# A two-layer cross-attention and expert network: padded tails, no mask matmul in the second scores, and a new order of steps

## The reference

```python
x = x + L0_xattn(layernorm(x), ctx)            # 16 heads of 8, over all 1601 keys
x = x + L0_ffn(layernorm(x))                   # 9 experts of width 352, top 2 of sigmoid scores
x = x + L1_xattn(layernorm(x), ctx, indices)   # 64 indices a query, values 0..255
x = x + L1_ffn(layernorm(x))                   # 8 experts of width 176 (top 2) + a shared one
```

## Time and profile before

| | us |
|---|---|
| median of 3 runs (lowest, highest) | 1853.64 (1852.64, 1859.54) |
| the profiled execution | 1856.58 |
| its span, first to last instruction | 1854.6 |
| PE busy in the span | 1582.5 (85%) |
| DVE, ACT, POOL busy | 1103.3, 805.9, 738.4 |
| mean granted TensorE clock, share of full speed | 0.92 |

### The profile page before, as it was taken

One profiled execution on the slowest core, in us unless ns is written; L12 is line 12 of the kernel. 1 busy time (PEld: TensorE's weight loads), 2 busy tenths in 40 slices (PEclk: granted clock), 3 DMA queues, 4 the chain that ended last, 5 costly groups with the idle time before them and its releaser, 6 DMA issues.

```text
span 1854.6 us, 34408 instructions
## 1 busy us (share of the span) xinstructions
PE 1582.5 (85%) x12939; PEld 869.8 (47%) x13006; DVE 1103.3 (59%) x2509; ACT 805.9 (43%) x1214; POOL 738.4 (40%) x1145
## 2 busy tenths in 40 slices
PE   3289798889988898889998898889988798899667
PEld 3133363346633574336633574345733465347425
DVE  3276476546766576556766476655766477655323
ACT  2146426651366425671366524661266524672211
POOL 0336305741178214771168313771058412750140
PEclk8589799988999999999999999997999999999757
DMA  6310300022000300012000200012000200000000
GB/s 196 64 39 28 89 1 1 27 48 46 1 10 19 67 26 1 18 38 50 15 10 20 67 26 1 18 34 44 26 1 28 56 15 1 2 14 4 1 0 3
DMA packets 64853, 53.65 MB, mean 29 GB/s; under 512 B 14762, under 2 KB 57140, under 8 KB 64692
## 3 DMA queue, kind: packets, MB, share of 16 engines
q1 hardware_dynamic: 64692, 51.47, 11.4%
HBM read 38.98 MB, written 12.46 MB: 28 GB/s over the span
## 4 chain that ended last, share of the span: by engine, by line
PE 63%; DVE 10%; POOL 10%; ACT 5%; issue 5%; SPq 4%; DMA 3%; POOLq 0%; ACTq 0%; DVEq 0%
PE um L671 12%; PE um L660 9%; PE ob L604 8%; PE um L661 7%; PE um L576 5%; DVE mx L1022 4%; PE um L591 4%; POOL big L1236 3%; PE um L554 3%; DMA kst<-k_parts 2%; DVE mx L1127 2%; ACT probs L846 2%; PE um L645 2%; SPq L498 1%; PE um L712 1%
## 5 line engine op out<-in xcount | busy, mean ns | idle before, releaser
L1022 DVE TENSOR_REDUCE mx<-um 128x2 f32<-128x802 f32 (+1 forms) x512 | 504.9, 991 | 228.4 <-PE um L576 220.9
L846 ACT ACTIVATE probs<-um 128x1024 f32<-128x1024 f32 (+1 forms) x448 | 426.6, 963 | 228.0 <-PE um L591 221.6
L852 ACT ACTIVATE hid<-um 128x256 f32<-128x256 f32 (+3 forms) x328 | 125.5, 383 | 503.7 <-PE um L661 503.6
L604 PE MATMUL ob<-probs,vaug 128*9 128x256 f32 (+1 forms) x3328 | 286.9, 394 | 12.4 <-ACT oT L822 12.2
L1201 POOL TENSOR_TENSOR big<-iotab,idx_lo 128x512 bf16<-128x512 bf16 x256 | 266.0, 1055 | 14.7 <-PE um L748 9.5
L576 PE MATMUL um<-kst,qa 64*128 64x401 bf16 (+1 forms) x1024 | 184.2, 359 | 63.6 <-DMA kst<-k_parts 38.1
L1164 POOL CAST qst<-nm 128x4 bf16<-128x4 f32 x64 | 17.1, 268 | 470.9 <-DVE nm L1028 470.4
L591 PE MATMUL um<-big,kst 64*128 64x256 bf16 (+1 forms) x1664 | 173.0, 281 | 16.5 <-ACT big L892 4.6
L1040 DVE SCALAR_TENSOR_TENSOR x<-um,cw,x 128x128 f32<-128x128 f32 x288 | 87.7, 346 | 126.2 <-PE um L671 126.2
L1034 DVE TENSOR_TENSOR hid<-hid,um 128x256 f32<-128x256 f32 (+3 forms) x328 | 133.5, 412 | 24.2 <-ACT hid L852 22.8
L576 PEld LDWEIGHTS um<-kst,qa 64*128 64x128 bf16 x1024 | 50.1, 95 | 202.3 <-issue 65.8
(11 more groups left out here) (209 smaller groups left out, 2265.1 us busy)
## 6 DMA issues: line engine op xcount, KB each, us to landing
kst<-k_parts SPq DMA_DIRECT2D x384, 50.0 KB
k_parts<-big SPq DMA_DIRECT2D x72, 128.0 KB, 1.9
ctx_sb<-in_ctx SPq DMA_DIRECT2D x8, 768.0 KB
k1st<-k_parts SPq DMA_DIRECT2D x96, 32.0 KB
k_parts<-big SPq DMA_DIRECT2D x24, 64.0 KB, 1.6
kst<-in_L_ffn_w SPq DMA_DIRECT2D x1, 1408.0 KB
x<-in_x SPq DMA_DIRECT2D x8, 128.0 KB, 2.2
out<-x SPq DMA_DIRECT2D x8, 128.0 KB, 1.9
```

The source lines that it names most:

```text
L604: m = pe.matmul(ob[q:q + V1, 0:NQ], vaug[b % 2][0:kn, c, 2 * p + hh, :], probs[0:kn, (2 * (NGB * b + g) + hh) % NPS, (c % 2) * NQ:(c % 2 + ...
L846: act.activation(probs[0:kn, k:k + 2, 0:w], own_banks, ACT.Exp).then_inc(f_read, 1)
L852: act.activation(hid[0:nr, own % NHID, :], quarter[place[ev][0]][0:nr, 0:NQ], ACT.Silu).then_inc(th_ready, 1)
L1022: dve.tensor_reduce(mx[:, p % 2, s, :, j], pair[:, :, 0:w], AX, ALU.max, negate=True).then_inc(u_read, 1)
```

## The change

It has three parts. The second network's down projections read all 128 rows: `wd_sb` gets 9 tail slots in place of 5, zeros are written to them first (a DVE memset), the tail of an even expert stands in rows 0 to 47 and that of an odd one in rows 64 to 111 of its own slot; chunks are all 128 rows wide; `NHID` falls from 10 to 8. The mask matmuls of `s1` go; instead `mu` takes the minimum of exp and 3e38 and multiplies by the count (zero for rows not named) in one instruction, which DVE does and not POOL; `msk` no longer waits for the `s1` of the batch before. And the positions come from a table: R is 88.94; of batch 0 the first 8 `part` stand early and the others among its `s0`; the early `part` of later batches start at 54.3 (before: 56.4); the late ones stand 1.2 apart (before 1.34), each behind an `s0`; `key` 4 moves to 48.10 and `rel` 0 to 2 to 47.97, so that they change places on SP; the pairs of the last batch stand 1.495 apart.

```diff
-NEG = -1e30
+NEG, BIG = -1e30, 3e38
-NHID = 10
+NHID = 8
+AT = {'cl': 0.75, 'cl1': 0.75, 'y1': -0.803, 'turn': 2.997, 'early': 32, 'first': 8, 'side': 1, 'p0': -0.922, 'p0s': 1.05, 'pf': -2.88, 'pfs': 0.697, 'px': 0.0, 'pxs': 1.201, 'psn': 0.1, ...
...
-        wg_sb, wu_sb, wd_sb = (sb(n, [P, NE + NT1, P]) for n in ("wg_sb", "wu_sb", "wd_sb"))
+        wg_sb, wu_sb, wd_sb = (sb(n, [P, NE + k, P]) for n, k in (("wg_sb", NT1), ("wu_sb", NT1), ("wd_sb", NE)))
...
-            return P if e < NE else (SLOT + TAIL if 2 * (e - NE) + 1 < NE else TAIL)
+            return P
...
-            o = SLOT * (e % 2)
-            tail = NE + e // 2
-            return [(len(chunk0) + chunk1.index((1, e, 0)), 0, P, e), (len(chunk0) + chunk1.index((1, tail, 0)), o, o + TAIL, tail)]
+            return [(len(chunk0) + chunk1.index((1, k, 0)), 0, P, at) for k, at in ((e, e), (NE + e // 2, NE + e))]
...
+            def part_at(b, k):
+
+                own, prep = R * b, R * (b - 1)
+                if b == 0:
+                    return prep + Y1 + AT["p0"] + 0.5 * k if k < FIRST else own + AT["pf"] + AT["pfs"] * (k - FIRST)
+                if k < EARLY:
+                    return prep + Y1 + AT["p0"] + AT["p0s"] * (k - k % SIDE)
+                t = AT["px"] + AT["pxs"] * (k - EARLY)
+                return own + t - t % 1.0 + AT["psn"]
...
-                    put(prep + (48 if c < 3 else XL + 1.5), "rel", b, c)
+                    put(prep + (AT["rel"] if c < 3 else XL + AT["rel3"]), "rel", b, c)
...
-                    put(prep + Y1 + 1.4 + EARLY_STEP * k if k < EARLY else own + (43.0 / (NH0 - EARLY)) * (k - EARLY) + 0.1, "part", b, k)
+                    put(part_at(b, k), "part", b, k)
...
-                put(own + 46.5, "key", b, 4)
+                put(own + AT["kk1"], "key", b, 4)
...
+                step = AT["pair"] if b < NB - 1 else AT["pairl"]
                 for p in range(NP):
-                    for d, kind in ((0, "pair1"), (2.05, "q1"), (3.05, "s1"), (3.6, "mu"), (6.05, "w1"), (7.05, "c1")):
-                        put(chain + 8.7 + 4.4 * p + d, kind, b, p)
+                    for kind in ("pair1", "q1", "s1", "mu", "w1", "c1"):
+                        put(chain + AT["pair0"] + step * p + AT[kind], kind, b, p)
...
-                    sp.dma_start(wd_sb[SLOT * h:SLOT * h + TAIL, NE:NE + 4, :],
+                    sp.dma_start(wd_sb[SLOT * h:SLOT * h + TAIL, NE:NE + 8, :].rearrange("p (k h) d -> p k h d", h=2)[:, :, h, :],
...
-                for hh in range(2):
-                    pe.matmul(own[hh], identb[:, :], maskT[:, :, :].rearrange("p c q -> p (c q)"), start=True, stop=False)
...
-                                      start=False, stop=(c == KC1 - 1))
+                                      start=True, stop=True)
...
+            dve.memset(wd_sb[:, NE:2 * NE, :], 0.0).then_inc(pre_dve, 1)
...
-                    if b >= 1:
-                        dve.wait_ge(f_psum, fill["s1", b - 1, NP - 1] + 1)
...
+                elif kind == "mu":
+                    k = (2 * n) % 4
+                    dve.wait_ge(f_read, fill["s1", b, n] + 1)
+                    dve.scalar_tensor_tensor(out=probs1[:, k:k + 2, :], in0=probs1[:, k:k + 2, :], scalar=BIG,
+                                             in1=cntT[b % 2].rearrange("p c q -> p (c q)").unsqueeze(1).to_broadcast([P, 2, 512]),
+                                             op0=ALU.min, op1=ALU.mult).then_inc(mulp, 1)
...
-                elif kind == "mu":
-                    k = (2 * n) % 4
-                    pool.wait_ge(f_read, fill["s1", b, n] + 1)
-                    pool.tensor_tensor(probs1[:, k:k + 2, :], probs1[:, k:k + 2, :],
-                                       cntT[b % 2].rearrange("p c q -> p (c q)").unsqueeze(1).to_broadcast([P, 2, 512]), ALU.mult).then_inc(mulp, 1)
```

More of the change, by code:

```diff
@@ L64 @@
 MMAX = 512
+AT = {'cl': 0.75, 'cl1': 0.75, 'y1': -0.803, 'y0': 0.0, 'turn': 2.997, 'early': 32, 'first': 8, 'side': 1, 'p0': -0.922, 'p0s': 1.05, 'pf': -2.88, 'pfs': 0.697, 'px': 0.0, 'pxs': 1.201, 'psn': 0.1, 'ldx': 2.094, 'ldc': 2, 'ctx': 4.4, 'ctxs': 3, 'key': 20.43, 'keys': 6, 'val': 2.2, 'vals': 1.96, 'rel': 47.968, 'rel3': 1.46, 'n4': 35.113, 'n4a': 36.446, 'xT4': 40.132, 'pq0': 45.745, 'idx': 52.742, 'lat': 14.821, 'all0': 50.579, 'all0s': 0.854, 'q00': -0.128, 'q0': -4.134, 'w0': 2.3, 'ev0': 1.4, 'c0': 2.45, 'dfs': 1.5, 'df': 0.6, 'eq': 4.381, 'cnt': 5.6, 'kk1': 48.096, 'kv1': 48.342, 'nm0': 2.7, 'aT0': 3.214, 'o0': 4.1, 'n1': 4.281, 'n1a': 5.081, 'xT1': 6.1, 'gate0': 7.0, 'le0': 8.1, 'rt0': 8.969, 'msk': 9.063, 'mq': 12.923, 'hd': 0.663, 'dn0': 2.2, 'dn1': 2.2, 'n2': 0.003, 'n2a': 1.906, 'xT2': 2.248, 'pq1': 2.606, 'all1': 5.709, 'pair0': 8.718, 'pair': 4.232, 'pairl': 1.495, 'pair1': -0.133, 'q1': 2.167, 's1': 3.149, 'mu': 3.717, 'w1': 5.642, 'c1': 7.454, 'nm1': 47.4, 'aT1': 48.3, 'o1': 48.455, 'n3': 49.3, 'n3a': 50.245, 'xT3': 51.385, 'gate1': 52.3, 'le1': 53.2, 'rt1': 55.07}
 def rows(c, total):
@@ L277, in build @@
         SERIAL = ("key", "n4a", "n1a", "n2a", "n3a", "le0", "le1")
[L279 to L284, removed]
+        XL = 56.0
+        CL, C1 = AT["cl"], AT["cl1"]
+        Y1 = XL + AT["y1"]
+        Y0 = Y1 + C1 * len(chunk1) + AT["y0"]
+        R = Y0 + CL * len(chunk0) + AT["turn"]
+        EARLY, FIRST = int(AT["early"]), int(AT["first"])
+        SIDE = int(AT["side"])
         def order():
@@ L318, in order @@
                 for n in range(P // QG):
-                    put(own + 1.5 * n + 0.6, "df", b, n)
+                    put(own + AT["dfs"] * n + AT["df"], "df", b, n)
                 for n in range(NCNT):
-                    put(own + 3 * n + 4.1, "eq", b, n)
-                    put(own + 3 * n + 5.6, "cnt", b, n)
-                put(own + 46.5, "key", b, 4)
[L324 to L328, removed]
+                    put(own + 2 * AT["dfs"] * n + AT["eq"], "eq", b, n)
@@ L329, in order @@
+                    put(own + 2 * AT["dfs"] * n + AT["cnt"], "cnt", b, n)
+                put(own + AT["kk1"], "key", b, 4)
+                put(own + AT["kv1"], "kv1", b)
+                for kind in ("nm0", "aT0", "o0", "n1", "n1a", "xT1", "gate0", "le0", "rt0", "msk", "mq"):
+                    put(own + XL + AT[kind], kind, b)
                 for u in range(len(chunk0)):
                     put(own + Y0 + CL * u, "gu", b, u)
-                    put(own + Y0 + CL * u + 0.8, "hd", b, u)
+                    put(own + Y0 + CL * u + AT["hd"], "hd", b, u)
@@ L332, in order @@
                 for e in range(NE):
-                    put(own + Y0 + CL * (J0 * e + 2) + 2.2, "dn", b, e)
-                for d, kind in ((0.8, "n2"), (1.9, "n2a"), (2.4, "xT2"), (3.3, "pq1")):
-                    put(chain + d, kind, b)
+                    put(own + Y0 + CL * (J0 * e + 2) + AT["dn0"], "dn", b, e)
+                for kind in ("n2", "n2a", "xT2", "pq1"):
+                    put(chain + AT[kind], kind, b)
                 for n in range(2):
-                    put(chain + 6.8 + 0.7 * n, "all1", b, n)
+                    put(chain + AT["all1"] + 0.7 * n, "all1", b, n)
@@ L343, in order @@
+                for kind in ("nm1", "aT1", "o1", "n3", "n3a", "xT3", "gate1", "le1", "rt1"):
+                    put(chain + AT[kind], kind, b)
                 for v in range(len(chunk1)):
-                    put(chain + Y1 + CL * v, "gu", b, len(chunk0) + v)
-                    put(chain + Y1 + CL * v + 0.8, "hd", b, len(chunk0) + v)
+                    put(chain + Y1 + C1 * v, "gu", b, len(chunk0) + v)
+                    put(chain + Y1 + C1 * v + AT["hd"], "hd", b, len(chunk0) + v)
                 for e in range(NE):
@@ L347, in order @@
                     v = chunk1.index((1, e, 0))
-                    put(chain + Y1 + CL * v + 2.2, "dn", b, NE + e)
-                put(chain + Y1 + CL * (len(chunk1) - 1) + 2.3, "out", b)
+                    put(chain + Y1 + C1 * v + AT["dn1"], "dn", b, NE + e)
+                put(chain + Y1 + C1 * (len(chunk1) - 1) + AT["dn1"] + 0.1, "out", b)
             at.sort(key=lambda v: (v[0], v[1]))
@@ L830, in _ @@
             act.wait_ge(w2_in, 16 * 8)
-            act.wait_ge(pre_dve, 10)
+            act.wait_ge(pre_dve, 11)
             for ev in EV:
```

35 lines of the change are left out of this document (17 added, 18 removed).

## The result

The changed kernel takes 1638.45 us (median of 4 runs, 1635.58 to 1640.13); the kernel before took 1856.59 in the same comparison. The ratio is 0.882, with an interval of 0.878 to 0.885. The changed kernel was timed in this comparison alone; the kernel before was timed again beside each group of experiments, with medians from 1848.83 to 1856.61 us.

The account below looks back on a forecast made before the run. PE, busy for 85% of the span, was taken as the main bound, less surely in attention. Terms summed to -156 us from the profiled 1856.6; less 2.9 to the median, that gave 1698 us, range 1650 to 1780.

Parts of the forecast that it names:

- Padded tails: Second network's down projections: 72 of them each lose 0.78 us of alternating 128 and 48 rows, -56 us (-35 to -65).
- No mask: Second scores in the attention stages: 0.54 us of PE per pair goes for 56 pairs, taken as -25 us (0 to -35).
- `rel` ahead of `key` 4: SP's queue at changes of round: kst reads issue earlier, so PE's waits for them go, -31.6 us (-10 to -31.6).
- clock, -15: Half-clock stretches beginning at the kst waits, 85.3 us together: up to 42.6 could come back, taken as -15 us.
- `mu`, -10.5 and +14: Multiply moved from POOL to DVE: PE's waits in the rounds go, -10.5 us; DVE's added work costs +14 (0 to +69).
- Last pairs, -26: Last batch's pairs, 64 us: a step of 4.0 us in place of 7.76 gives 38 us, so -26 (-16 to -34).
- First round, -6: Batch 0: 24 early maxima move behind the first s0, which starts some 14 us sooner; net -6 us (+5 to -15).
- Other positions, 0 within 15: Remaining steps move by up to two positions with no stage losing its cover: 0 us, bounds +15 and -15.
- DVE as the limit: Rival: DVE becomes the attention stage's limit, mask and POOL-wait gains vanish and DVE adds 56 us: 1775 us, chance 0.15.
- Another wait in place of the one for `kst`: Rival at the change of round: PE waits for something else late and the clock still falls: 1745 us, chance 0.14.
- Loose pairs: Rival in the last pairs: each pair waits for the whole one before, so the 26 us stay: 1724 us, chance 0.05.
- The slower case: Rival in attention stages: exp waits in DVE's stream starve PE and drop its clock: about 1876 us, chance 0.03.

Follow-up runs that it names:

- the masked kernel: The changed kernel with the two mask matmuls of each second score back, and msk's wait for the s1 of the batch before: 1666.86 us, ratio 0.901.

## Why the prediction was wrong in size

Step by step, in its own order:

- *Padded tails, -56*: -56 alone and 56 when taken back. Right.
- *No mask, -25*: 26 to 33 when taken back at the same clock, the last pairs included. About right there, but not secure: the execution with masks at a clock of 0.96 is only 4 us slower than the changed kernel's median, and in the old order, without masks and with the multiply on DVE, the attention stages fell by 10 us where this term and the two of `mu` had 21.5.
- *`rel` ahead of `key` 4, -31.6, and clock, -15*: the exchange alone brought 56, 9 more than the two. Right in kind; the waits fell by 34.2 us, so the clock's part was too small: the 72 us less at half clock are worth up to 36. In the changed kernel, half-clock time at the changes of round fell from 85.3 us to 10.2. In the new order the exchange is a condition for the earlier maxima and worth 88.
- *`mu`, -10.5 and +14*: the operation takes 1.22 us, as sized, and PE waits 4.1 us for it. (Of the 28.0 us before, the last pairs hold 19.0, not 17.5, which leaves 9.0 for the rounds.) But the term looked at the multiply alone. What counts is what it does to the rest of POOL's stream, the splits of the maxima above all, for which the change is worth up to 93 us once the order is dense.

```profile
L1137 DVE SCALAR_TENSOR_TENSOR big<-big,cntT x32: 1210/1216/2095, 289.1 to 1478.5; 128x1024 f32<-128x1024 f32 x32
```

- *Last pairs, -26*: the stretch shrank by 41 us, of which 5 to 7 are the last network; taking the spacing back costs 21, because the multiply on DVE alone had shortened the pairs from 53.0 to 45.0. The step length was oversized: (1590.1 - 1571.7) / 7 = 2.6 us, below my bound of 2.9, with a clock of 0.81 in place of the 0.53 that I had kept; DVE is busy for 18.4 of those 22 us.
- *First round, -6*: 10 when taken back. About right.
- *Other positions, 0 within 15*: **this step failed.** It said that no stage loses its cover; it didn't ask what a stage gains. The priced parts without those positions and without the first round run at 1698.32, and the positions bring 60 more. Of these the early start of batch 0 is 10, which the sum had as its first round; the other 50 stood at zero. The place behind an `s0` is 22 of them and the density 14, each measured by taking it back; the rest, some 14, wasn't separated (the larger distance before a round, the shorter ones inside a pair, the moved transposes). Why a denser stream pays is open, as is half of the 22.

That the forecast of 1698 is the time of that kernel is in part luck: the exchange was sized 9 too small, the last pairs 5 too large, and the mask with `mu` brought less than half of its terms in the attention stages when it stood alone.

Of the rivals, DVE as the limit is refuted where it was strongest: with 80 of 110 us in the attention stage DVE makes PE wait 18.0 us for the pairs' maxima in the whole run, in 14 waits of at most 2.3, and a thinner stream of maxima is slower. Another wait in place of the one for `kst` did not come: PE is busy for 28.0 of 28.0 us. Loose pairs did not come either. The slower case had the right mechanism on the wrong engine: late work starves PE and its clock falls, but from POOL's load (0.86 with idle work on it), not from DVE's waits.

`mu` takes 1.22 us at the median and 2.10 at the longest. The Trainium skill (GPSIMD Engine Reference, Key points) says that POOL and DVE share SBUF interfaces and contend when the DVE instruction has two SBUF inputs. The trace agrees: the longest `mu`, 2.10 us, starts 0.14 us behind a POOL product of 1.16 us. POOL is held too, as the last section shows. It cost little here, since POOL's long multiply, which had stretched an `eq` to 2.44 us, went: the longest is now 1.27.

```profile
L1075 DVE TENSOR_SCALAR big<-big x128: 410/418/1272, 106.1 to 1490.5; 128x1024 bf16<-128x1024 bf16 x128
```

## What to carry to other kernels

Where one engine is nearly full and fed by three in-order streams, the order of steps and the load of the feeders can't be priced one after the other: with the multiply on POOL (85 of 122 us) the new positions made the seven attention stages 15 us longer, with it on DVE (69 of 110) the positions are worth 60 us. When a diff moves many positions, price the changes of matmul tile shape that it saves or adds (count the neighbours), and ask which feeder's slack a denser order will spend. Look in the DMA queue's own order for loads that could have been issued earlier: exchanging two steps was worth as much as rewriting the down projections.

## What the runs showed of the hardware

A matmul whose tile takes 48 rows between matmuls of 128 rows costs 0.2 us at each change (8 instructions in 1.67 us against 0.89), while 96 rows between 128 cost nothing; the four changes in one projection account for the 0.78 us. I had read this from the trace, and the padding confirms it. The changes between 64-row scores and the 128-row products of `w0` cost half as much, 0.1 us each.

Not expected: a POOL instruction is held by a DVE instruction with two SBUF inputs, to its end. A subtraction of 4 columns takes 0.20 us, and 1.13 while `mu` (1.23 us on DVE) runs beside it, in the timeline of the last pairs:

```profile
1579.63 1.23 DVE L1137 SCALAR_TENSOR_TENSOR big<-big,sq_nat 128x1024 f32<-128x1024 f32 x1
1579.79 1.13 POOL L1179 TENSOR_TENSOR nmr<-mx,big 128x4 f32<-128x4 f32 x1
```

Also not expected was how far the granted clock differs between stages that are nearly equally busy: the attention stage of batch 2 was granted 0.97, 0.92, 0.90 and 0.86 in four kernels with 14, 10, 16 and 15 us of idle PE time in 110 to 122. So the idle sum alone doesn't give the clock, and the runs don't settle what does. The spread of the masked kernel, 1642 to 1673 us with its clock at 0.96 to 0.94, shows that the same program can be granted either.
